# Spreading the row-maximum products of a softmax-attention kernel over the whole block, with five moved one block ahead

## The reference

```python
# layer 0: non-local attention on the group-normalised x
q = prelu(conv1x1(x, w1, b1), a1)      # 24 channels
k = prelu(conv1x1(x, w2, b2), a2)      # 24 channels
v = prelu(conv1x1(x, wa, ba), aa)      # 192 channels
score = softmax(einsum('bnc,bcm->bnm', q, k), axis=2)   # 4096 x 4096 an image
out = einsum('bnm,bmc->bnc', score, v)
x = x + out
# layer 1: a likelihood model, channel by channel, on the group-normalised x
lower, upper = logits_cumulative(x - 0.5), logits_cumulative(x + 0.5)
x = x + maximum(abs(sigmoid(sign * upper) - sigmoid(sign * lower)), 1e-6)
```

## Time and profile before

| what | value |
|---|---|
| median of 3 runs | 4865.89 us (4865.57 to 4873.28) |
| the profiled execution's own time | 4868.1 us |
| its span | 4866.3 us |
| PE busy | 4460.5 us, 92% |
| DVE busy | 4178.8 us, 86% |
| ACT busy | 3717.8 us, 76% |
| POOL busy | 937.5 us, 19% |
| mean granted PE clock | 0.982 of full speed |

### The profile page before, as it was taken

The page is one execution under the profiler, slowest core; times in us unless marked ns, Lnnn a source line. Parts: engine busy times, 40 slices in busy tenths (PEclk is TensorE's granted clock), DMA queues, the critical chain, the costliest instruction groups (busy, mean ns, idle before and its releaser), DMA issues.

```text
span 4866.3 us, 107519 instructions
## 1 busy us (share of the span) xinstructions
PE 4460.5 (92%) x38780; PEld 2978.2 (61%) x38780; DVE 4178.8 (86%) x5433; ACT 3717.8 (76%) x4214; POOL 937.5 (19%) x937
## 2 busy tenths in 40 slices
PE   6999989999899998999899998999989999899976
PEld 4888347773477725777257762678617785277821
DVE  6897899978999798996999969899698987989866
ACT  2776887768877697776977769777797777977787
POOL 4200202212122111221112120121202212022112
PEclk9999999999999999999999999999999999999988
DMA  2001421114211142111412023120332113311133
GB/s 66 25 20 30 100 70 47 34 39 105 62 47 40 36 110 51 47 40 46 108 45 57 28 62 98 39 58 27 77 86 60 36 38 73 96 42 34 38 88 95
DMA packets 154989, 279.95 MB, mean 58 GB/s; under 512 B 37441, under 2 KB 37921, under 8 KB 152706
## 3 DMA queue, kind: packets, MB, share of 16 engines
q1 hardware_dynamic: 154434, 272.69, 21.8%
HBM read 205.24 MB, written 50.33 MB: 53 GB/s over the span
## 4 chain that ended last, share of the span: by engine, by line
PE 57%; DVE 17%; issue 13%; ACT 12%; DMA 1%; DVEq 0%; ACTq 0%; SPq 0%; POOL 0%; POOLq 0%
PE ps L1486 10%; PE ps L1488 10%; PE ps L1490 10%; PE ps L1261 7%; DVE mxp L1164 6%; PE ps L1438 6%; ACT th L777 5%; ACT arena L770 5%; DVE arena L1058 4%; PE ps L1360 3%; PE ps L1294 3%; DVE th L1096 3%; PE ps L1346 3%; PE ps L1318 2%; PE ps L1253 1%
## 5 line engine op out<-in xcount | busy, mean ns | idle before, releaser
L1486 PE MATMUL ps<-v_sb,arena 128*128 128x193 f16 x8192 | 2017.5, 246 | 18.4 <-DVE arena L1058 18.4
L1488 PE MATMUL ps<-v_sb,arena 128*128 128x192 f16 x8192 | 2026.6, 247 | 0.0
L1490 PE MATMUL ps<-v_sb,arena 128*128 128x193 f16 x8192 | 2009.6, 245 | 0.0
L732 ACT ACTIVATE arena<-ps 128x1024 f16<-128x1024 f32 x1024 | 1049.9, 1025 | 773.8 <-PE ps L1261 772.8
L1058 DVE TENSOR_TENSOR arena<-arena 128x1024 f16<-128x1024 f32 x1024 | 1346.1, 1316 | 258.4 <-ACT arena L735 258.3
L1164 DVE TENSOR_REDUCE mxp<-ps 128x1 f32<-128x512 f32 x1792 | 1162.2, 683 | 32.5 <-PE ps L1438 24.8
L1096 DVE SCALAR_TENSOR_TENSOR th<-th,gates,ps 128x1024 f32<-128x1024 f32 x768 | 949.9, 1275 | 148.7 <-ACT th L777 141.4
L735 ACT ACTIVATE arena<-ps 128x1024 f32<-128x1024 f32 x1024 | 1046.4, 1022 | 0.2 <-DVE arena L1058 0.2
L1488 PEld LDWEIGHTS ps<-v_sb,arena 128*128 128x128 f16 x8192 | 794.8, 97 | 261.8 <-issue 0.3
L777 ACT ACTIVATE th<-ps,biases 128x1024 f32<-128x1024 f32 x768 | 826.1, 1120 | 119.9 <-PE ps L1346 81.5
L1486 PEld LDWEIGHTS ps<-v_sb,arena 128*128 128x128 f16 x8192 | 792.0, 97 | 150.5 <-issue 28.6
(11 more groups left out here) (147 smaller groups left out, 3448.3 us busy)
## 6 DMA issues: line engine op xcount, KB each, us to landing
x<-x2d SPq DMA_DIRECT2D x1152, 64.0 KB, 2.4
arena<-x2d SPq DMA_DIRECT2D x768, 64.0 KB, 2.5
xp<-x_dram SPq DMA_DIRECT2D x18, 1536.0 KB, 10.1
shared<-x_dram SPq DMA_DIRECT2D x64, 384.0 KB, 3.7
x2d<-shared SPq DMA_DIRECT2D x64, 384.0 KB, 3.0
res<-x2d SPq DMA_DIRECT2D x96, 256.0 KB
out_dram<-res SPq DMA_DIRECT2D x96, 256.0 KB
kst<-shared SPq DMA_DIRECT2D x32, 256.0 KB, 3.3
```

The lines of the kernel that those rows point to most:

```text
L732: act.activation(e_hi[:, q % 4, :].rearrange("p (k n) -> p k n", k=2), sc, ACT.Exp)
L1486: pe.matmul(acc, eh, v_sb[:, m, 0:C + 1], start=(m == 0 and t % 2 == 0), stop=False, skip_group_check=True)
L1488: pe.matmul(acc[:, 0:C], eh, v_sb[:, m, VW:VW + C], start=False, stop=False, skip_group_check=True)
L1490: ins = pe.matmul(acc, el, v_sb[:, m, 0:C + 1], start=False, stop=(m == MT - 1), skip_group_check=True)
```

## The change

Per image there are as many maxima as before. Five of the 32 for block j+2 are now made in block j, in p13 (one), p14 and p15 (two each), for j up to 5 (`early_tiles`). The other 27 follow in the next block, two and three a pair in turns, in p0 to p10. Block 0 keeps its own 32, four a pair, and gets five early ones for block 2; block 6 has only 27.

Since the early products use the banks into which the next block accumulates, PE waits at that block's start until all five are reduced. The ordinary ones that come first (5 and 6) wait for `out_norm`. The bank of product m is now (m + 1) % 2. To free the banks earlier, `turn_parts` moves from the ends of p12 and p13 to those of p11 and p12, and `add_half` from p13 and p14 to p12 and p13; the first early product in each bank waits for the residual addition that has read it.

```diff
-PER_STEP = 3
+EARLY_AT = {13: [0], 14: [1, 2], 15: [3, 4]}
+EARLY = 5
+PER_PAIR = [2, 3, 2, 3, 2, 3, 2, 3, 2, 3, 2]
...
 def max_tiles(p, first):
-    per, begin = (4, 3) if first else (PER_STEP, 0)
-    return list(range(max(per * (p - begin), 0), min(max(per * (p - begin + 1), 0), MAXES)))
+    if first:
+        return list(range(max(4 * (p - 3), 0), min(max(4 * (p - 2), 0), MAXES)))
+    begin = EARLY + sum(PER_PAIR[:p])
+    return list(range(begin, begin + PER_PAIR[p])) if p < len(PER_PAIR) else []
+
+
+def early_tiles(j, p):
+
+    return EARLY_AT.get(p, []) if j + 2 < BLOCKS else []
...
-                    dve.tensor_reduce(mxp[:, m // BLOCKS, m % BLOCKS:m % BLOCKS + 1], ps[:, bank + m % 2, :],
+                    dve.tensor_reduce(mxp[:, m // BLOCKS, m % BLOCKS:m % BLOCKS + 1], ps[:, bank + (m + 1) % 2, :],
...
-                        if not first and p in (13, 14):
-                            add_half(b, j - 1, p - 13)
+                        if not first and p in (12, 13):
+                            add_half(b, j - 1, p - 12)
+                        for m in early_tiles(j, p):
+                            reduce(dve.compute_val(maxes + MAXES), m, free)
...
                     if m >= 2:
                         pe.wait_ge(max_red, base + (m - 1))
-                    elif evacuated is not None:
+                    if evacuated is not None and m in (EARLY, EARLY + 1):
                         pe.wait_ge(out_norm, evacuated + START)
...
                         if p == 0 and not first:
                             pe.wait_ge(x2_ready, b * 2 * BLOCKS + 2 * (j - 1) + START)
+                            if not last:
+                                pe.wait_ge(max_red, maxes + EARLY)
...
-                        spots = (1, 3, 5, 7) if first else (5, 6, 7) if p == 0 else (2, 5, 7)
+                        spots = (1, 3, 5, 7) if first else (5, 7) if p == 0 else (2, 5, 7) if len(todo) == 3 else (3, 7)
+                        ahead = early_tiles(j, p).copy()
...
+                                if i * NT + t in ((6,) if p == 13 else (4, 7)) and ahead:
+                                    if ahead[0] < 2 and first:
+                                        pe.wait_ge(max_rows, blocks + 2)
+                                    elif ahead[0] < 2:
+                                        pe.wait_ge(x2_ready, b * 2 * BLOCKS + 2 * (j - 1) + ahead[0] + 1 + START)
+                                    max_tile(pe.compute_val(maxes + MAXES), q_next + N, ahead.pop(0), free, None)
+                        assert not todo and not ahead
+                        if not first and p in (11, 12):
+                            if p == 11:
                                 pe.wait_ge(out_split, b * (BLOCKS - 1) + j)
+                                if not last:
+                                    pe.wait_ge(max_red, maxes + MAXES)
                             elif not last:
                                 pe.wait_ge(max_rows, blocks + 2)
-                            turn_parts(j - 1, p - 12)
+                            turn_parts(j - 1, p - 11)
```

More of the change, by code:

```diff
@@ L1435, in max_tile @@
                         pe.wait_ge(max_red, base + (m - 1))
-                    elif evacuated is not None:
+                    if evacuated is not None and m in (EARLY, EARLY + 1):
                         pe.wait_ge(out_norm, evacuated + START)
-                    pe.matmul(ps[:, bank + m % 2, :], qst[:, q_col + m // BLOCKS * P:q_col + (m // BLOCKS + 1) * P],
+                    pe.matmul(ps[:, bank + (m + 1) % 2, :], qst[:, q_col + m // BLOCKS * P:q_col + (m // BLOCKS + 1) * P],
                               kst[:, (m % BLOCKS) * N:(m % BLOCKS + 1) * N], start=True, stop=True
@@ L1495, in phase_b @@
                                     max_tile(maxes, q_next, todo.pop(0), free, None if first else blocks)
-                        if not first and p in (12, 13):
-                            if p == 12:
+                                if i * NT + t in ((6,) if p == 13 else (4, 7)) and ahead:
[7 more added lines that the diff above has]
+                            if p == 11:
                                 pe.wait_ge(out_split, b * (BLOCKS - 1) + j)
+                                if not last:
+                                    pe.wait_ge(max_red, maxes + MAXES)
                             elif not last:
                                 pe.wait_ge(max_rows, blocks + 2)
-                            turn_parts(j - 1, p - 12)
+                            turn_parts(j - 1, p - 11)
                 pe.wait_ge(full_ready, pairs + PAIRS)
```

## The result

| | before | changed |
|---|---|---|
| median of 8 runs each | 4869.14 us | 4886.51 us |
| range | 4865.57 to 4873.96 | 4883.81 to 4891.51 |
| ratio, 95% interval | | 1.0036 [1.0026, 1.0047] |
| span of the profiled execution | 4866.3 us | 4888.2 us |

What follows compares the result with a forecast made beforehand. TensorE was taken as the bound, with only 2.75 us of waits to win in a tail block; new waits and savings over all blocks summed to +26 us on the median 4865.9, giving 4892 us, range 4860 to 4914.

Steps and rivals of the forecast that it cites:

- The gate: Start of blocks 1 to 6: first accumulation waits for early maximum 4's reduction, until 1.15 after the old block's last matmul; +0.50 us.
- The banks: Spot 5 of p0: a later reciprocal delays ACT's copies that free the banks; +0.68 us behind a result, +0.08 in image 0.
- Pair 2's hold: End of p1, blocks 1 to 6: POOL's L690 holds pair 2's subtraction 0.68 us; PE waits 0.53 instead of 0.21.
- p3: End of p3, tail blocks: the subtraction is still held until POOL's L588 ends; PE waits 0.84 rather than 0.63, +0.21 us.
- p4, p8 and the turn: Tail blocks: two maxima in p4 and p8 remove waits, -0.49 and -0.40; out-transposes before the maxima's turn in p12, -0.44 us.
- Tail block: Block with tails of the previous image's second layer, 35 of blocks 1 to 5: all terms together +0.3 us.
- Image 0's blocks: Blocks 1 to 5 of image 0, without tails: +0.96 us each.
- Blocks 0 and 6: Block 0 has five more maxima, +1.08 us; block 6 five fewer, +0.39 behind a tail block, -0.2 in image 0.
- A: Rival: POOL's instructions fall beside reductions, so holds of pair 2 and p3 vanish; 55 us off, 4837, faster; chance 0.10.
- B: Rival: only pair 2's subtraction escapes POOL's L690; 25 us off, 4867, no change; chance 0.18.
- C: Rival: late copies delay ACT's exponentials, a second PE stop in p2, about 0.5 us in each of 48 blocks; 4916; chance 0.11.

Runs made afterwards that it cites:

- the last version: All four repairs on the changed kernel, second result behind p13, POOL's sum ahead of split_out's second half: 4790.37 us, 0.9842 of the kernel before.

## Why the prediction was right, and where it was off

**The gate, +0.50.** Right: PE's first accumulation is at 1537.82, T+1.17, where I had T+1.15. Moving only its cause (spots 2 and 5) took it away.

**The banks, +0.68 and +0.08.** Right: the maximum at spot 5 starts at 1539.97 = T+3.32, released by ACT's copies, computed T+3.33. Moving only the result took 0.53 of it away.

**Pair 2's hold, +0.53.** Right in size and cause: 1.89 us for the subtraction, 3.43 for the window of p2, and 2.87 with POOL's instruction moved away. In image 0 it cost 0.45.

**p3, +0.21.** Right: the subtraction took 2.26 instead of 2.04, and the load's idle time at the end of p3 grew from 0.71 to 0.92. The window of p4 is 3.75 as before, although it holds one product fewer; with POOL's difference moved away it is 2.87.

**p4, p8 and the turn, -0.49, -0.40, -0.44.** Right: the windows of p5 and p9 fell from 3.60 and 3.50 to 3.08, and the idle time before the turn from 1.10 to 0.66. The transposes alone gave 0.43 on the kernel before.

**The sums.** Tail block: forecast +0.3, measured +0.27. Image 0's blocks: forecast +0.96, measured +0.76 (3.8 us for five). Here the term of pair 2 was over-sized by 0.08. The first of these blocks grew by only 0.5: POOL is still at other work there, its second half of the split starts at T+7.5 instead of T+3.7, and the window of p2 is 2.87, without a hold. The forecast priced this block like the other four. Blocks 0 and 6: forecast +1.08 and +0.39, measured +0.87 (from p13 on) and +0.60 behind a tail block. The step that failed is the place of the fifth early product: it is issued behind the last accumulation, so its 0.21 us belong to the next block; together the two are right. Image 0's block 6 has a slip in the sum: its terms give 0.96-1.08 = -0.12, not -0.2; measured -0.08. In all 26 us were forecast; the blocks moved 23.8, the profiled span 21.9, the median 17.4. So of the nearly 9 us by which the forecast is too high, about 2 are in its terms, 2 lie outside the blocks, and 4.5 are the distance of the two profiled executions from their medians. What lies between the blocks varied from 1450 to 1458 us for the seven gaps over these twelve profiles, with no order that follows the changes; the forecast took it as unchanged. The terms miss in both directions: blocks 0 by -2.1 us, image 0's by -1.0, tail blocks by about -1, blocks 6 by +1.5. That the sum comes within 2 to 3 us of the blocks' +23.8 is partly luck; that each wait has its place and size is not.

**The rivals.** A and B, in which POOL's instructions miss the subtractions, didn't occur of themselves; made to occur one at a time, each gave about what was priced: 27 us for pair 2 (priced at 25) and 23 for p3 (29). C, a second stop in p2, did not occur: p3's window is 3.08.

Where the expected gain of the change went is thus shown: it won 0.49 + 0.40 + 0.44 us a tail block and lost 1.7 in the new waits of p0 and p1, against 0.3 there before, and 0.21 in p3. With the waits repaired, one by one, the same spread is 1.6% faster. Not all of this is the spread's: the wait of p3 was in the kernel before too (0.63 us a tail block), and so was a small hold of pair 2. No run puts the two waits on POOL and the earlier result on the kernel before, so what they would give there, without the spread, stays open.

## What to carry to other kernels

Work that is brought forward into the last moments of a stage lands ahead of the steps that hand over to the next one: list what stands behind it on each in-order engine (here the reciprocal, and through it ACT's copies and the banks), and measure the hand-over from the point at which the stage ends. Before adding a repair, ask which idle time it uses; two that work alone may need the same gap. And where two engines exclude each other, move the long instruction beside work that doesn't care, or give the pair behind the collision less to do.

## What the runs showed of the hardware

A DVE subtraction with both inputs in SBUF that starts while a POOL `tensor_tensor` reads SBUF ends as if it had started 0.14 us before that one's end: 2.26 us at 1548.23 beside POOL's 1548.15 to 1549.42, and 1.89 at 1541.78 beside 1540.94 to 1542.59 (undisturbed it takes 1.22). In the changed kernel the 0.14 is the same in all 42 collisions with POOL's `lu<-lu`. It works the other way round too: 42 times POOL's multiplication (`lu<-lu,lu_sign`, 1.27 us alone) starts during a subtraction there and ends 1.12 to 1.13 us after it. The Trainium skill ("SBUF — State Buffer", section "Who interferes with whom") says that a VectorE instruction with two SBUF inputs contends with a GpSimd instruction that reads SBUF, and that this is an exclusive lock; this case agrees up to the 0.14. It also says that a VectorE `tensor_reduce` never contends on trn2. Three reductions beside POOL's 1.65 us took 1.97, with waits for their products in it; in the changed kernel 187 reductions lie wholly beside a POOL instruction, and each takes 0.68 to 0.69 us, as the others do.

How far a delay of POOL can be moved at little loss is seen in the last version, where its sum and both held instructions stand elsewhere:

```profile
1512.00 1.26 POOL L591 TENSOR_TENSOR lu_sign<-lu 128x512 f32<-128x512 f32 x1
...
1512.95 1.39 DVE L1075 TENSOR_TENSOR arena<-arena 128x1024 f16<-128x1024 f32 x1
...
1521.99 2.07 DVE L1075 TENSOR_TENSOR arena<-arena 128x1024 f16<-128x1024 f32 x1
```

POOL's long operations still meet the subtractions of pairs 2 and 5, which take 1.39 and 2.07 us. The short hold of pair 2, ahead of three reductions, costs PE 0.06; the long one of pair 5, ahead of two, costs 0.14 (window of p6). In the changed kernel the long hold of pair 4, ahead of three, costs 0.87.
